# The head's last layer on three engines: two bias additions on GpSimd, the row normalisation on ScalarE

## What is computed

```python
mod = (_silu(c) @ wmod).reshape(8, 6, 1, -1)          # sa, ca, ga, sb, cb, gb
h = _layernorm(x) * (1 + ca) + sa
x = x + ga * _attn(h)                                  # three iterations, 16 heads
h = _layernorm(x) * (1 + cb) + sb
x = x + gb * _ffn(h)        # _ffn: blocks of 32 onto a 6-bit grid, @ wd.T + bias
```

## Time and profile before

| | |
|---|---|
| median of 3 runs | 358.79 us (358.68 to 359.64) |
| the profiled execution, its own time | 358.5 us |
| its span in the profile | 356.7 us |
| mean granted TensorE clock | 0.976 |
| busy: TensorE | 320.0 us, 90% |
| busy: VectorE | 284.8 us, 80% |
| busy: GpSimd | 240.6 us, 67% |
| busy: ScalarE | 239.4 us, 67% |

### The profile page before, as it was taken

How to read it: one execution, slowest core, us unless ns; L and a number is a source line. 1 busy time by engine, 2 the same in 40 slices (tenths; PEclk the granted TensorE clock), 3 DMA queues, 4 the chain that set the end, 5 groups by cost and what they waited for, 6 DMA issues and landing times.

```text
span 356.7 us, 6296 instructions
## 1 busy us (share of the span) xinstructions
PE 320.0 (90%) x2247; PEld 243.4 (68%) x2247; DVE 284.8 (80%) x498; ACT 239.4 (67%) x537; POOL 240.6 (67%) x142
## 2 busy tenths in 40 slices
PE   7997984958999989998999999979999989994994
PEld 5223653748998777786788778767887768673883
DVE  4899839947727997969898879797878989899832
ACT  3357463577968798789788899876779897231410
POOL 2339956059876896989599979984999499702000
PEclk9999998798999999999999999989999999999899
DMA  6999899972697097958698977597837962020122
GB/s 207 395 405 367 277 214 234 314 237 112 120 218 197 2 239 204 222 152 217 183 242 265 242 136 291 154 233 158 257 120 152 233 180 115 6 86 31 73 105 88
DMA packets 23797, 68.51 MB, mean 192 GB/s; under 512 B 2467, under 2 KB 2596, under 8 KB 19798
## 3 DMA queue, kind: packets, MB, share of 16 engines
q1 hardware_dynamic: 16224, 53.40, 43.8%
q0 software_dynamic: 7392, 14.68, 24.9%
q10 hardware_dynamic: 150, 0.02, 0.0%
HBM read 50.96 MB, written 17.14 MB: 191 GB/s over the span
## 4 chain that ended last, share of the span: by engine, by line
PE 38%; DVE 25%; ACT 16%; POOL 9%; issue 9%; DMA 1%; SPq 0%; DVEq 0%; POOLq 0%; ACTq 0%
PE ps L747 7%; PE ps L748 7%; PE ps L752 7%; ACT U L501 5%; PE ps L730 4%; ACT unused L514 3%; DVE XL L1184 3%; PE ps L832 3%; POOL U L390 3%; DVE DD L1234 2%; DVE Q L1227 2%; DVE amax L1208 2%; ACT XH L469 2%; DVE X L1241 2%; POOL U L397 2%
## 5 line engine op out<-in xcount | busy, mean ns | idle before, releaser
L747 PE MATMUL ps<-WH,XH 128*128 128x512 f32 x256 | 108.4, 424 | 6.0 <-DVE X L1241 4.2
L748 PE MATMUL ps<-WL,XH 128*128 128x512 f32 x256 | 102.4, 400 | 0.0
L390 POOL TENSOR_TENSOR U<-U,c_bc 128x1024 f32<-128x1024 f32 x31 | 76.4, 2466 | 19.7 <-ACT U L501 19.6
L397 POOL TENSOR_TENSOR U<-U,sb_bc 128x1024 f32<-128x1024 f32 x31 | 74.2, 2394 | 4.5 <-POOL U L390 0.2
L1184 DVE TENSOR_TENSOR XL<-ps,XH 128x512 fp32r<-128x512 f32 x64 | 43.9, 685 | 40.4 <-ACT XH L469 40.3
L752 PE MATMUL ps<-WH,XL 128*128 128x512 f32 x256 | 69.4, 393 | 1.5 <-DVE XL L1184 1.5
L469 ACT ACTIVATE XH<-ps 128x512 fp32r<-128x512 f32 x64 | 37.5, 586 | 47.5 <-PE ps L730 47.3
L501 ACT ACTIVATE U<-X,nmr,rstd 128x512 f32<-128x512 f32 x64 | 48.2, 807 | 28.6 <-DVE nmr L1201 26.0
L747 PEld LDWEIGHTS ps<-WH,XH 128*128 128x128 f32 x256 | 49.7, 194 | 17.1 <-DVE X L1241 5.4
L752 PEld LDWEIGHTS ps<-WH,XL 128*128 128x128 f32 x256 | 48.6, 190 | 12.7 <-DVE XL L1184 1.9
L748 PEld LDWEIGHTS ps<-WL,XH 128*128 128x128 f32 x256 | 49.8, 195 | 8.8
(11 more groups left out here) (232 smaller groups left out, 443.8 us busy)
## 6 DMA issues: line engine op xcount, KB each, us to landing
X<-in_x SPq DMA_DIRECT2D x16, 1024.0 KB, 7.5
out<-X SPq DMA_DIRECT2D x15, 1024.0 KB, 6.0
X<-mod_scratch POOLq DMA_DIRECT2D x14, 1024.0 KB, 13.6
X<-in_wmod SPq DMA_DIRECT2D x2, 1024.0 KB, 12.2
sb_bc<-mod_scratch SPq DMA_DIRECT2D x7, 256.0 KB, 12.9
c_bc<-mod_scratch SPq DMA_DIRECT2D x7, 256.0 KB, 11.2
gb_bc<-mod_scratch SPq DMA_DIRECT2D x6, 256.0 KB, 5.7
X<-in_wmod SPq DMA_DIRECT2D x2, 512.0 KB, 4.7
```

Source lines behind the costliest of these rows:

```text
L390: nc.gpsimd.tensor_tensor(a, a, spread(c_bc[:, b % 2, :]), ALU.mult).then_inc(u_done, 2 if g == 0 else 1)
L397: nc.gpsimd.tensor_tensor(a, a, spread(sb_bc[:, b % 2, :]), ALU.add).then_inc(h_done, 2 if g == 0 else 1)
L747: M(bank, XH[:, n % 2, r], WH[:, b % 2, k, :], start=k == 0, stop=False)
L748: M(bank, XH[:, n % 2, r], WL[:, b % 2, k, :], start=False, stop=False)
```

## The change

Three pieces of the head's last layer move. GpSimd multiplies `row_bc` (the output bias) by msp row 2 (the gate) and adds the product to `xs`, the head's rows of x, ahead of the product with Wo, at a new place, `head_bias`; at its very end it adds msp row 0 (gate times bias of the second layer). ScalarE does the normalisation into the bank `bb`, for which VectorE prepares 1/std and -mean/std in slot 56. VectorE keeps gate, residual, moments, modulation and grid. ScalarE's root of the variance moves from slot 56 to slot 55. Semaphores are renamed and merged (`u_first` and `h_first` to `first_h`, and so on), with the counts adapted.

```diff
@@ GpSimd
+            def head_bias():
+                pool.wait_ge(hs_done, 1)
+                pool.wait_ge(bo_in, 32)
+                pool.wait_ge(msp2_in, 2 * 16 * B)
+                nc.gpsimd.tensor_tensor(row_bc[:], row_bc[:], msp[:, 2, :], ALU.mult).then_inc(xs_step, 1)
+                pool.wait_ge(xs_step, 1)
+                nc.gpsimd.tensor_tensor(xs[:], xs[:], row_bc[:], ALU.add).then_inc(xs_step, 1)
...
                 if g == 1:
                     centre_diagonals()
+                if g == GROUPS - 3:
+                    head_bias()
             from_grid(GROUPS - 1)
+            pool.wait_ge(norm_done, 1)
+            nc.gpsimd.tensor_tensor(xs[:], xs[:], msp[:, 0, :], ALU.add).then_inc(xs_step, 1)
@@ ScalarE
+                elif q == AFTER + 4:
+                    norm_std(2)
                 elif q == AFTER + 5:
-                    norm_std(2)
+                    act.wait_ge(sxd_done, 1)
+                    A.activation(bb, xs[:], ACT.Identity, bias=st[:, 5, 2:3], scale=st[:, 3, 2:3]).then_inc(norm_done, 1)
@@ TensorE
                 elif q == AFTER + 7:
-                    pe.wait_ge(sxd_done, 1)
+                    pe.wait_ge(sxd_done, 2)
@@ VectorE
                 elif q == AFTER + 4:
                     dve.wait_ge(proj_mm, 1)
-                    dve.wait_ge(bo_in, 32)
-                    dve.wait_ge(msp2_in, 2 * 16 * B)
-                    link(TT(bb, bb, row_bc[:], ALU.add))
+                    dve.wait_ge(xs_step, 2)
                     link(TT(bb, bb, msp[:, 2, :], ALU.mult))
                     link(TT(xs[:], xs[:], bb, ALU.add))
                     moments(xs[:], 2)
                 elif q == AFTER + 5:
-                    normal(bb, xs[:], 2)
+                    dve.wait_ge(norm_done, 1)
                     link(TT(bb, bb, msp[:, 3, :], ALU.mult))
                     link(TT(hs[:], bb, msp[:, 4, :], ALU.add))
                 elif q == AFTER + 6:
                     quantise(hs[:].unsqueeze(1), Qh[:].unsqueeze(1), NB).then_inc(sxd_done, 1)
-                    link(TT(xs[:], xs[:], msp[:, 0, :], ALU.add))
...
                 elif q == AFTER + 11:
                     dve.wait_ge(sy_mm, 1)
                     link(TT(bb, bb, msp[:, 1, :], ALU.mult))
+                    dve.wait_ge(xs_step, 3)
                     TT(xs[:], xs[:], bb, ALU.add).then_inc(head_out, 1)
...
                 if q + 1 < LAST:
                     low_part(q + 1)
+                if q == AFTER + 5:
+
+                    dve.wait_ge(std_done, 3)
+                    link(REC(st[:, 3, 2:3], st[:, 1, 2:3]))
+                    TS(st[:, 5, 2:3], mv[:, 0:1], st[:, 3, 2:3], -1.0, ALU.mult, ALU.mult).then_inc(sxd_done, 1)
```

More of the change, by code:

```diff
@@ L185, in build @@
         (ga_mm, cs_mm, rows_mm, rows_cp, gate_mm, v_row, cs_rows, gb_col, rows_turned, columns_cp,
-         columns_out, cs_out, g_rows, u_first, h_first, xd1_done, s32_done) = (
+         columns_out, cs_out, g_rows, first_h, xd1_done, s32_done) = (
             sem(n) for n in (
                 "ga_mm", "cs_mm", "rows_mm", "rows_cp", "gate_mm", "v_row", "cs_rows", "gb_col",
[L189 to L192, removed]
+                "rows_turned", "columns_cp", "columns_out", "cs_out", "g_rows", "first_h", "xd1_done", "s32_done"))
+        bd_done, hs_sa, bdm_done, w_grid, gb_in, xs_step, norm_done, plain_cp, w_copied = (
+            sem(n) for n in ("bd_done", "hs_sa", "bdm_done", "w_grid", "gb_in", "xs_step", "norm_done", "plain_cp", "w_copied"))
         (exp_c, silu_done, mod_mm, wd_done, wscaled, wt_mm,
@@ L204, in build @@
              "attT_cp", "proj_mm", "sxd_done", "sxT_mm", "sxh_cp", "sxl_done", "sy_mm", "head_out"))
-        (ksum_done, lrs_done, lg_done, lmax_done, esum_done, einv_done, diff_done, keep_done, att_done,
+        (ksum_done, lrs_done, lg_step, e_step, diff_done, keep_done, att_done,
          dn_step) = (sem(n) for n in (
-             "ksum_done", "lrs_done", "lg_done", "lmax_done", "esum_done", "einv_done", "diff_done",
+             "ksum_done", "lrs_done", "lg_step", "e_step", "diff_done",
              "keep_done", "att_done", "dn_step"))
@@ L602, in _ @@
             normalise(0, 1)
-            act.wait_ge(u_first, 1)
+            act.wait_ge(first_h, 1)
             A.copy(c_bc[:, 0, :], ps[:, C_BANK, :]).then_inc(cs_rows, 1)
@@ L607, in _ @@
             A.copy(column_rows, ps[0:COLUMNS * B, COLUMN_ROWS, :]).then_inc(columns_cp, 1)
-            act.wait_ge(h_first, 1)
+            act.wait_ge(first_h, 2)
             A.copy(sb_bc[:, 0, :], ps[:, S_BANK, :]).then_inc(cs_rows, 1)
@@ L1031, in first_modulate @@
                 dve.wait_ge(cs_mm, 1)
-                TT(a, spread(C_BANK), a, ALU.mult).then_inc(u_first, 1)
-                dve.wait_ge(u_first, 1)
+                TT(a, spread(C_BANK), a, ALU.mult).then_inc(first_h, 1)
+                dve.wait_ge(first_h, 1)
                 dve.wait_ge(cs_mm, 2)
-                TT(a, a, spread(S_BANK), ALU.add).then_inc(h_first, 1)
+                TT(a, a, spread(S_BANK), ALU.add).then_inc(first_h, 1)
             def spread(bank):
@@ L1077, in attend @@
                        st[:, 4, 0:16].rearrange("p (c q) -> p q c", q=4).unsqueeze(3).to_broadcast([P, 4, NC, 32]),
-                       ALU.mult).then_inc(lg_done, 1)
+                       ALU.mult).then_inc(lg_step, 1)
                     flat = lg.rearrange("p q c t -> p (q c) t")
-                    dve.wait_ge(lg_done, i + 1)
-                    RED(lmax, flat, AX, ALU.max).then_inc(lmax_done, 1)
-                    dve.wait_ge(lmax_done, i + 1)
+                    dve.wait_ge(lg_step, 2 * i + 1)
+                    RED(lmax, flat, AX, ALU.max).then_inc(lg_step, 1)
+                    dve.wait_ge(lg_step, 2 * i + 2)
                     TT(flat, flat, wide16(lmax), ALU.subtract).then_inc(sub_done, 1)
@@ L1087, in attend @@
                                  ex.rearrange("p q c t -> p (q c t)")).then_inc(eT_done, 1)
-                    RED(st[:, 6, 0:16], ex.rearrange("p q c t -> p (q c) t"), AX, ALU.add).then_inc(esum_done, 1)
-                    dve.wait_ge(esum_done, i + 1)
-                    REC(st[:, 7, 0:16], st[:, 6, 0:16]).then_inc(einv_done, 1)
+                    RED(st[:, 6, 0:16], ex.rearrange("p q c t -> p (q c) t"), AX, ALU.add).then_inc(e_step, 1)
+                    dve.wait_ge(e_step, 2 * i + 1)
+                    REC(st[:, 7, 0:16], st[:, 6, 0:16]).then_inc(e_step, 1)
                 elif o == 12:
-                    dve.wait_ge(einv_done, i + 1)
+                    dve.wait_ge(e_step, 2 * i + 2)
                     dve.wait_ge(pv_mm, i + 1)
@@ L1204, in maxima @@
                 if g == 0 and h == 0:
-                    dve.wait_ge(h_first, 1)
+                    dve.wait_ge(first_h, 2)
                 else:
```

## The result

The changed kernel takes 365.35 us (median of 4 runs, 364.18 to 366.12) against 359.22 us for the kernel before in the same runs (358.68 to 361.11): ratio 1.0158, 95% interval 1.0110 to 1.0206. The forecast was 364.5, range 362.9 to 366.4. The profiled execution took 364.18 with a span of 362.4; the forecast span was 362.5.

What follows compares the result with a forecast made beforehand. Bound by TensorE up to Wo's product, then ScalarE and VectorE, then TensorE from the head's transposes. 6.9 lost less 1.1 won is +5.8 on 358.5, so 364.3 profiled; 0.3 more for the median gives 364.5, range 362.9 to 366.4.

Steps and rivals of the forecast that it cites:

- The wait and its place: GpSimd's head_bias waits for msp transfers until 290.1, ahead of group 14's modulation; VectorE's second maxima come 6.9 us late.
- the other end: The last msp transfer lands at 291.1 instead of 290.1, a bound of +1.0 us.
- The sign "about 3.5 us": On VectorE, the first of two waits before group 14's maxima, ended by GpSimd, would show as about 3.5 us.
- Not amplified: GpSimd finishes group 15's second half at 319.5, VectorE wants it at 320.4: 0.9 us early, so the delay does not grow.
- What is won: Work taken off VectorE in slots 55 and 56 lets the head's transposes start 1.1 us earlier.
- The last addition: Adding msp row 0 (0.68 us) moves from VectorE to GpSimd; hidden behind the head's transposes before, so it gives nothing.
- The clock: TensorE's clock falls at product 52, hidden inside the wait for att; nothing added, 1.4 us kept as the other end.
- rival 1: TensorE's clock also falls behind the wait for att's transposes: 1.4 us more, 365.9 us, chance 0.15.
- The sum: At the end of the kernel, 6.9 us lost less 1.1 us won: +5.8 us, median 364.5, 1.6% slower.
- that the wait is hidden: Rival: head_bias's wait on GpSimd fits the slack and the change gains 1.1 us, to 357.7 us; chance 0.04.
- that ScalarE's reordering costs more: Rival: ScalarE's new order holds up more than a high part, so the 1.1 is not won; 365.7 us, chance 0.08.
- that the delay is caught up: Rival: TensorE's idle places behind 310 us absorb part of the delay; 362.5 us, chance 0.08.

Runs made afterwards that it cites:

- e1: The change with head_bias moved on GpSimd from the iteration for group 13 to behind group 15; 357.97 us, ratio 0.9960 against the kernel before.
- e3: As e1, plus two idle 128x512 products on GpSimd at the change's place for head_bias; 356.68 us, ratio 0.9939 against the kernel before.
- e4: The change with SyncE issuing row_bc and the large msp transfers first, head_bias waiting for those alone; 362.23 us, ratio 1.0084 against the kernel before.
- e2: The kernel before with only head_bias, at the change's place; normalisation, root and last addition as before; 365.98 us, ratio 1.0188.
- e5: The change without head_bias, the bias addition on VectorE again; 359.25 us, ratio 0.9994 against the kernel before.
- e6: As e1, with the root of the variance back in ScalarE's slot 56; 357.40 us, ratio 0.9954 against the kernel before.
- e7: As e6, with the addition of msp row 0 on VectorE again; 358.02 us, ratio 0.9962 against the kernel before.
- e8: As e6, with e3's two idle products on GpSimd ahead of group 14; 356.99 us, ratio 0.9947 against the kernel before.

## Why the prediction was right, point by point

- **The wait and its place.** Forecast: transfers landed at 290.1, group 14 at 292.9, second maxima 6.9 late. Measured: 290.11, 292.86, 6.6. e1 and e3 show that without this wait nothing is lost, e4 that the loss follows the landing one to one once the slack of 4.96 us is used up, e2 that head_bias alone makes it all. That the landing agrees so closely is luck: the last issue came at 285.37 instead of 284.8, and that transfer took 4.74 us instead of 5.3, and the two misses cancel. In e2 the landing came 1.1 us later against the issues, near the other end I had kept. The wake-up of 0.1, for which the prediction has no row, was 0.16 in the change (290.11 to 290.27). The sign "about 3.5 us" for VectorE's first wait was a slip: the forecast's own times give 4.5 (297.9 less 293.36), and 4.22 was measured.
- **Not amplified.** Forecast: group 15 in time by 0.9. Measured: 0.9. ScalarE waited 3.19 us for image 7's first scaled weights, not about 1, since the high part ahead of that wait was through at 302.60, sooner than I had it; it had caught up before TensorE needed anything.
- **What is won.** Forecast 1.1, by terms 0.72 (the bias addition), 1.04 (normalisation), less 0.34 (the root ahead of a high part) and 0.31 (two small instructions). Measured: 1.18 in all (e1 against before); 0.74 for the bias addition (e5 against e1, 38.39 less 37.65), 0.32 for the root (e6 against e1), and 0.44 for normalisation, root and small instructions together (e5) against 0.39.
- **The last addition.** Forecast: moved for nothing. That step holds for the kernel before, at the lower clock, but not in general: at the upper clock it is worth 0.5 us (e7, and e2 with the same wait). It was mis-sized as 0 where it is 0 to 0.5.
- **The clock.** Forecast: down at product 52, hidden, not at att's transposes. So it was: product 52's first matmul took 0.80 us, and the product ended at 304.50, inside the wait for att. The Trainium skill ("TensorE: Matmul & The Clock Gate", section "HAM oscillation — how this bites in real kernels") tells of a kernel with waits of about 3 to 5 us that pays the return to the full clock after each of them. Behind the 1.59 us wait here it was not paid, behind e4's 3.01 us it was, and it was paid behind most of the waits of 2.73 to 2.78 us too. But the prediction's ground, that the wait of 2.08 us had done no harm, was weaker than it looked. In e2 the same wait, 2.06 us, was followed by the lower level within product 58, and only the wait for the quantiser behind it hid that:

```profile
333.66 0.50 PE L757 MATMUL ps<-WH,XH 128*128 128x512 f32 x1 [2.06 <-DVE X L1249]
...
334.99 0.63 PE L757 MATMUL ps<-WH,XH 128*128 128x512 f32 x1
```

That rival 1 did not come to pass in the change was in part luck. So was the tail: the change's execution held 1.6 us of lower clock there (26.62 against e3's 24.98), the one before 1.4, so it fell out of the difference but for 0.3 us. The prediction took that for granted; e3 and e7 show that the clock can stay up behind the same wait.
- **The sum.** 6.6 - 1.2 = 5.4 us make the delay at the head's transposes (5.45 measured); with 0.3 behind them it is 5.7 on the span, 5.8 forecast. The median of the runs rose by 6.1.

The rivals: that the wait is hidden is refuted by the traces of the change and of e2; that ScalarE's reordering costs more by e5; that the delay is caught up by the change's own trace.

## What to carry to other kernels

Before an operation moves to an engine with idle time, ask when its operands have landed, not only whether the time is free: here GpSimd had 4.7 idle microseconds at the new place and the work would have fitted (e3), but its rows landed 14 us later, and in an in-order queue everything behind stood still. The transfers had cost nothing before, because their consumer came 24 us after the landing. Once the work stood where its rows had long been there (e1), the same change was a gain, ratio 0.9960 (0.9938 to 0.9981); with the root moved back as well (e6) it was 0.9954 (0.9931 to 0.9978).

## What the runs showed of the hardware

- Nine of the ten traces have the same wait of 2.7 to 2.8 us for the head's quantiser. Behind it the granted clock stayed full in two (e3, e7), fell after 1.4 us or less in three (the change, e1, e5), fell at once for about 3 us in three (before, e4, e6) and stayed low for some 6 us in one (e8). In e3, the change, before and e8 the tail was 24.98, 26.62, 26.37 and 27.83 us. It is the largest spread between executions whose orders are nearly alike there, and larger than what e6 wins over e1.
- Shorter waits can be followed by the lower level too: in e2 it came within 1.4 us of the end of a wait of 2.06 us, where the kernel before stayed at the full clock behind 2.08 us.
- Sixteen transfers in a row took SyncE 9.2 to 10.0 us to issue in nine traces, with one issue of 1.6 to 2.0 us among them. The last landing came 13.6 us behind the first issue in the change and 14.7 in e2.
